# One VectorE operation for a row tile's 1448 scores instead of two in a decoder layer's cross-attention

## The reference, cut to what matters

```python
Q = (input_Q @ W_Q.T + b_Q)...            # 16 heads of 64
K = (input_K @ W_K.T + b_K)...            # 1444 keys
V = (input_V @ W_V.T + b_V)...
scores = jnp.einsum('bhqd,bhkd->bhqk', Q, K) / np.sqrt(D_K)
scores = jnp.where(attn_mask[:, None, :, :], -10000.0, scores)
attn = jax.nn.softmax(scores, axis=-1)
out = jnp.einsum('bhqk,bhkd->bhqd', attn, V)
```

## Time and profile before

| | us |
|---|---|
| median of 3 runs | 1603.62 |
| lowest, highest | 1602.78, 1609.25 |
| the profiled execution's own time | 1606.2 |
| its span, first to last instruction | 1604.5 |
| TensorE busy in the span | 1463.2 |
| VectorE busy | 1143.5 |
| ScalarE busy | 883.8 |
| GpSimd busy | 973.1 |

### The profile page before, as it was taken

One profiled execution on the slowest core, in us unless ns is written; L12 is line 12 of the kernel. 1 busy time (PEld: TensorE's weight loads), 2 busy tenths in 40 slices (PEclk: granted clock), 3 DMA queues, 4 the chain that ended last, 5 costly groups with the idle time before them and its releaser, 6 DMA issues. The chain is left out here.

```text
span 1604.5 us, 35506 instructions
## 1 busy us (share of the span) xinstructions
PE 1463.2 (91%) x10557; PEld 1408.8 (88%) x10557; DVE 1143.5 (71%) x2672; ACT 883.8 (55%) x1632; POOL 973.1 (61%) x1101
## 2 busy tenths in 40 slices
PE   4856999999999999999999999999999999956796
PEld 4736999999999999999999999999999999945585
DVE  5644878686878687868686868686868686768565
ACT  0303656565656565656565656565656565625453
POOL 2015858575857585757675767576757585414564
PEclk9956999999999999999999999999999999966898
DMA  7021111111111111111110111011101011024422
GB/s 164 1 68 62 54 34 52 35 50 35 52 35 50 35 52 35 50 36 50 35 55 31 52 34 55 31 54 32 55 31 55 30 33 35 8 65 113 113 61 88
DMA packets 98038, 80.76 MB, mean 50 GB/s; under 512 B 17577, under 2 KB 96530, under 8 KB 97714
## 3 DMA queue, kind: packets, MB, share of 16 engines
q1 hardware_dynamic: 88848, 71.83, 15.1%
q10 hardware_dynamic: 6882, 2.21, 1.0%
q0 software_dynamic: 2112, 4.29, 0.8%
HBM read 67.26 MB, written 11.04 MB: 49 GB/s over the span
## 5 line engine op out<-in xcount | busy, mean ns | idle before, releaser
L943 ACT CAST pT_hi<-banks 128x512 fp32r<-128x512 f32 (+1 forms) x672 | 360.9, 542 | 342.6 <-PE banks L1098 337.5
L1012 DVE TENSOR_TENSOR pT_lo<-banks,pT_hi 128x512 fp32r<-128x512 f32 (+1 forms) x576 | 358.2, 626 | 220.3 <-ACT pT_hi L943 212.4
L875 POOL TENSOR_SCALAR probs<-probs,row_inv 128x1408 f32<-128x1408 f32 x192 | 278.7, 1451 | 235.7 <-DVE row_inv L1004 235.4
L1098 PE MATMUL banks<-ident,probs 128*128 128x128 f32 (+1 forms) x2304 | 365.8, 274 | 5.3 <-POOL probs_half L877 3.2
L1128 PE MATMUL banks<-pT_hi,ctx_hi 128*128 128x256 f32 (+1 forms) x1056 | 329.5, 312 | 17.8 <-DVE pT_lo L1012 13.8
L863 POOL TENSOR_SCALAR bias<-mask,c_cur 128x1444 f32<-128x1444 uint8 x192 | 282.9, 1473 | 82.4 <-DVE nmax L997 64.3
L934 ACT ACTIVATE probs<-probs,nmax 128x1448 f32<-128x1448 f32 x192 | 289.8, 1509 | 39.0 <-DVE nmax L997 38.9
L1128 PE MATMUL banks<-pT_hi,ctx_lo 128*128 128x256 f32 (+1 forms) x1056 | 303.1, 287 | 0.0
L1128 PE MATMUL banks<-pT_lo,ctx_hi 128*128 128x256 f32 (+1 forms) x1056 | 302.4, 286 | 0.0
L1098 PEld LDWEIGHTS banks<-ident,probs 128*128 128x128 f32 (+1 forms) x2304 | 271.0, 140 | 17.0 <-DVE pT_lo L1012 9.0
L1082 PE MATMUL banks<-ctxT_hi,qh 128*128 128x362 f32 x832 | 241.9, 372 | 4.8 <-POOL ql L912 2.8
(11 more groups left out here) (287 smaller groups left out, 2339.9 us busy)
## 6 DMA issues: line engine op xcount, KB each, us to landing
mask<-in_mask_BxSxS_bk SPq DMA_DIRECT2D x192, 180.5 KB
nat<-in_ctx SPq DMA_DIRECT2D x16, 704.0 KB
up_raw<-in_L_ffn_W SPq DMA_DIRECT2D x32, 128.0 KB, 2.7
xs_dram<-empty SPq DMA_DIRECT2D x1, 2600.0 KB, 8.2
rows<-xs_dram SPq DMA_DIRECT2D x10, 260.0 KB, 3.0
down_raw<-in_L_ffn_W SPq DMA_DIRECT2D x16, 128.0 KB, 3.1
t_both<-yk_dram SPq DMA_DIRECT2D x3, 512.0 KB, 5.3
mask_half<-in_mask_BxSxS_bk SPq DMA_DIRECT2D x16, 90.2 KB
```

Source lines behind the costliest of these rows:

```text
L875: pool.tensor_scalar(prob(j)[0:n, 0:FIRST], prob(j)[0:n, 0:FIRST], rinv[0:n, s:s + 1], 1.0, ALU.mult, ALU.mult)
L943: act.copy(pT_hi[tslot(i, j)][:, 0:w], banks[:, T_BANK + j % 2, 0:w]).then_inc(turned_hi, 1)
L1012: dve.tensor_tensor(p_lo, turn, p_hi.bitcast(F32), ALU.subtract).then_inc(turned_lo, 1)
L1098: last = pe.transpose(banks[0:m, T_BANK + j % 2, at_col:at_col + 128], prob(t)[:, c0:c0 + m], ident[:, :])
```

## The change

`period()` puts both halves of a tile's scores next to each other, in the middle of a thirteenth of the period, instead of at even distances. `dve_order()` has one score operation per tile, at the place of the second half. It waits for the second half's scores, reads banks 0 to 3 in one instruction (four runs of 362), writes 1448 probabilities and the minimum at once, and raises `scores_taken` by 2. Nothing else is edited: ScalarE's exp waits for the same count and takes the same `nmax[:, 1]`. GpSimd's bias and normalizing keep their offsets from the halves.

```diff
@@ period()
-    for n in range(2 * NT):
-        out.append(((n + 0.5) / (2 * NT), "score", 0, n))
+    for t in range(NT):
+        for half in range(2):
+            out.append(((t + 0.5 + half / 1000) / NT, "score", 0, 2 * t + half))
@@ dve_order()
-        if kind == "score":
+        if kind == "score" and j % 2:
             out.append((n + 0.2, "score", db, j))
-            if j % 2:
-                out.append((n + 3.6, "recip", db, j // 2))
+            out.append((n + 3.6, "recip", db, j // 2))
@@ VectorE's program
                         if kind == "score":
-                            t, half = j // 2, j % 2
+                            t = j // 2
                             n, s = rows_of(t), slot(t)
-                            if half == 0:
-                                wait(dve, bias_ready, b + db, NT, t + 1)
...
+                            wait(dve, bias_ready, b + db, NT, t + 1)
...
-                            else:
-
-                                wait(dve, scores_taken, b + db, 2 * NT, j)
...
                             wait_apart(dve, scores_ready, b + db, 2 * NT, j + 1, passed_dve)
-                            cs = slice(half * 2 * CW, (half + 1) * 2 * CW)
-                            src = banks[0:n, S_BANK + 2 * half:S_BANK + 2 * half + 2, 0:CW]
-                            first = -PAD if half == 0 else nmax[0:n, 0, s:s + 1]
 
                             dve.tensor_tensor_reduce(
-                                prob(t)[0:n, cs].rearrange("p (a k) -> p a k", a=2), src,
-                                bias[(t + i) % 2][0:n, cs].rearrange("p (a k) -> p a k", a=2), -1.0, first,
-                                ALU.add, ALU.min, nmax[0:n, half, s:s + 1]).then_inc(scores_taken, 1)
+                                prob(t)[0:n, 0:SKP].rearrange("p (a k) -> p a k", a=4),
+                                banks[0:n, S_BANK:S_BANK + 4, 0:CW],
+                                bias[(t + i) % 2][0:n, :].rearrange("p (a k) -> p a k", a=4), -1.0, -PAD,
+                                ALU.add, ALU.min, nmax[0:n, 1, s:s + 1]).then_inc(scores_taken, 2)
```

More of the change, by code:

```diff
@@ L977, in emit @@
                         if kind == "score":
-                            t, half = j // 2, j % 2
+                            t = j // 2
                             n, s = rows_of(t), slot(t)
-                            if half == 0:
-                                wait(dve, bias_ready, b + db, NT, t + 1)
[L983 to L986, removed]
-                                else:
-                                    wait(dve, turned, b + db, NSTEP, steps_to(group_of(t + PSLOTS)) - NSTEP)
+                            wait(dve, bias_ready, b + db, NT, t + 1)
+                            if t >= FT:
+                                wait(dve, turned, b + db, NSTEP, 0)
+                            elif t >= PSLOTS:
+                                wait(dve, turned, b + db, NSTEP, steps_to(group_of(t - PSLOTS)))
                             else:
-                                wait(dve, scores_taken, b + db, 2 * NT, j)
+                                wait(dve, turned, b + db, NSTEP, steps_to(group_of(t + PSLOTS)) - NSTEP)
                             wait_apart(dve, scores_ready, b + db, 2 * NT, j + 1, passed_dve)
-                            cs = slice(half * 2 * CW, (half + 1) * 2 * CW)
-                            src = banks[0:n, S_BANK + 2 * half:S_BANK + 2 * half + 2, 0:CW]
-                            first = -PAD if half == 0 else nmax[0:n, 0, s:s + 1]
                             dve.tensor_tensor_reduce(
-                                prob(t)[0:n, cs].rearrange("p (a k) -> p a k", a=2), src,
-                                bias[(t + i) % 2][0:n, cs].rearrange("p (a k) -> p a k", a=2), -1.0, first,
-                                ALU.add, ALU.min, nmax[0:n, half, s:s + 1]).then_inc(scores_taken, 1)
+                                prob(t)[0:n, 0:SKP].rearrange("p (a k) -> p a k", a=4),
+                                banks[0:n, S_BANK:S_BANK + 4, 0:CW],
+                                bias[(t + i) % 2][0:n, :].rearrange("p (a k) -> p a k", a=4), -1.0, -PAD,
+                                ALU.add, ALU.min, nmax[0:n, 1, s:s + 1]).then_inc(scores_taken, 2)
                         elif kind == "recip":
```

## The result

The changed kernel takes 1827.37 us (median of 4 runs, 1825.18 to 1827.94), the kernel before 1603.6; the ratio is 1.138 [1.136, 1.141]. It was forecast slower at 1894, range 1800 to 1935: right in sign, 67 us too high.

What follows compares the result with a forecast made beforehand. TensorE's instruction stream bounds the kernel. 15 full periods at 18.5 us (277), plus 20 for the first batch, minus 7 at back edges: +290 on 1606.2 is 1896; the runs' median is 2.6 lower, 1894 us, range 1800 to 1935.

Steps and rivals of the forecast that it cites:

- The path: Attention stage: TensorE's stream sets the time; the chain score operation, exp, copy, subtraction, transpose has no slack.
- the walk: One period followed in the new order, each engine in order: TensorE waits at tiles 0 to 12 sum to 19.5 us.
- The three limits: After a tile's scores: next scores wait until 2.07 us, second-next step's transposes 2.76 (last group 2.56), one further 4.94 (4.58).
- The banks: Score banks between tiles: three steps (3.2 us) cover their 2.07 us; only tile 12 would wait, 0.15.
- The first batch: Its first four tiles have no steps beside them and wait 2.07 each: about 6, rest 14, together 20 us.
- One full period: Walk's 19.5 us less about 1 us of idle swallowed: 18.5 us per period, 15 periods, 277 us.
- the back edges: Loop's back edge: TensorE is absent 2.3 us anyway while others catch up, giving 7 x -1 us.
- About 1 us of today's idle: Each full period: idle already there that the new waits swallow, taken off the walk's 19.5 us.
- (a): Loop: granted clock falls, a tenth of TensorE's 78 us per period at 1.2 GHz; adds 60 to 120 us; chance 0.08.
- (b): Only the last group's tiles stall, preps' bank and pair waits hidden by slack: about 1700, 1650 to 1795 us; chance 0.08.
- (c): No change: three steps cover the bank wait and nothing else matters; 1595 to 1612 us, chance 0.01.
- (d): VectorE's saved 0.3 us per tile shortens what TensorE waits for: 1598 us, chance 0.01.

Runs made afterwards that it cites:

- experiment 1: Kernel before with only the new score order, both halves paired, keeping two VectorE operations per tile: 1834.94 us, 1.140.
- kernel 2: Changed kernel with the score halves back at the even distances of before, keeping the one long operation: 1759.31 us, 1.093.
- Experiment 3: Changed kernel with exp one place later in ScalarE's order: 1750.85 us, 1.085.
- experiment 5: Changed kernel with a score operation half as long, half the probabilities left out, ScalarE filled up by a copy of constants: 1701.68 us, 1.057.
- 11: Kernel before with halves paired, two operations per tile, and prep rounds 2, 5, 8 (6, 9) later: 1816.21 us, 1.129.
- 6: Changed kernel with halves 0.3 of a tile's share apart and exp one place later: 1686.59 us, 1.045.
- 10: Changed kernel with halves 0.3 of a share apart, exp one place later, and prep rounds 2, 5, 8 (6, 9) later: 1737.05 us, 1.076.
- 4: Changed kernel with the score halves 0.3 of a tile's share apart, exp as before: 1745.37 us, 1.086.
- 9: Kernel before with only exp one place later on ScalarE: 1642.46 us, 1.019.

## Why the prediction was right in direction and 67 us too high

**The path.** TensorE's stream was the bound and got longer by waits for subtractions queued on VectorE behind the operation and behind exp, as forecast. Which part of the change does it, the prediction left to its walk of the whole, and my reading of that walk, that it is the operation's length, isn't borne out: with the halves paired, two operations cost the same (experiment 1, 1.140 against 1.138).

**The operation:** 1.66 us forecast, 1661 ns measured. **VectorE's saving** was to be 60 us beside TensorE and worth nothing. It was worth nothing. The groups of the score operation and its reads add up to 423 us before (185.1 + 173.9, for the last tile 15.3 + 14.4, reads 31.9 + 2.4) and to 362 after (318.9, 26.4, reads 17), 60 less as forecast, while the busy union fell by 35 and the other groups kept their durations. So I take 25 us of the 60 to have been overlap: a read starts before its operation's end (702.37 + 0.97 = 703.34 against 703.26 in the earlier trace rows), and rows subtracted from a busy total take such overlap off twice.

**The three limits** were right where the rows show them: T + 2.07 for the release of exp and banks, T + 2.50 (2.56) for turn 39, T + 4.56 (4.58) for turn 40. **The banks** weren't the cost of the change (6.0 us), as steps in other banks stand behind the scores. The rule of the Trainium skill's Perfetto Trace Analysis (Optimizing Tensor Performance, Matmuls), that independent groups should rotate through banks, didn't decide the time here. That holds for this order alone: kernel 2 does wait for its banks, 94 us. **The first batch:** 20 forecast; the second batch's first scores start at 223.53 instead of 207.68 us, 15.8 later. (The 19.8 above is read a part of a period further on, at the projection, and is no measure of this term, close as it comes.)

**One full period: 18.5 forecast, 14.0 measured.** This is the term that was mis-sized, by 4.5 x 14 = 63 us. And there are 14 of them, not 15: the last batch has no preps for a next one beside it, and from its first scores (1534.74 instead of 1322.58 us) to the end of the span the change cost 9.1 us, where 18.5 was counted. Against these stand the 7 us that the back edges were to give back; the seven periods that hold one grew by 13.9, the seven others by 14.1, so they gave back 0.2 each. In sum 4.2 + 63 + 9.4 - 7 is 69 to 70 us, which is what the forecast of +290 had over the spans' 221.3.

Where in the period, I measured from the end of one tile's pair of scores to the start of the next, in a period away from the back edge, and set it beside the walk's (the unit times of what stands between, and the wait):

| after tile | measured | walk | | after tile | measured | walk |
|---|---|---|---|---|---|---|
| 0 | 5.60 | 5.7 | | 7 | 5.13 | 5.03 |
| 1 | 5.63 | 5.53 | | 8 | 6.14 | 6.76 |
| 2 | 4.85 | 4.83 | | 9 | 3.82 | 3.67 |
| 3 | 2.96 | 2.92 | | 10 | 5.58 | 6.08 |
| 4 | 6.56 | 6.84 | | 11 | 6.56 | 7.05 |
| 5 | 5.33 | 5.29 | | 12 | 2.11 | 2.76 |
| 6 | 4.58 | 4.57 | | | | |

Seven tiles agree within 0.1. (In the other period of a pass tile 0 has 6.1 to 8.2 and tile 12 mostly 2.9 to 3.7, since it holds the back edge.) The walk is too high at 8, 10, 11 and 12, by 2.3 in all, mostly where VectorE arrives late and the lateness is carried on. I had let each instruction start after the end of the one ahead; in the rows above two pT_hi copies of 0.43 take 0.73 together and two subtractions of 0.49 take 0.89, so queued instructions overlap by 0.1, and a chain of late ones catches up. That this is what made these four tiles shorter is argued, not shown. The other nine tiles cancel out (0.1), and a pair of halves took 2.08 instead of 2.14 (13 x 0.06 = 0.8): 3.0 found tile by tile.

The rest is in what I subtracted. "About 1 us of today's idle" was the busy share's gap in the earlier trace rows and the waits of the earlier trace rows. Unit times (an estimate) give another number: 26 halves 28.1, 30 steps of 256 columns, five of them shorter, 30.95, the last group's twelve 8.4, eleven preps 4.85, the projection 3.5; with 1.2 for the back edge 77.0. So the kernel before, at 80.0, idled about 3 us a period beside the back edge. And the walk's stalls on top of 77.0 give 96.5 where 93.0 was measured: the walk was 3.5 too high, of which the tiles above show 3.0. A busy union hides it, as the timeline of the kernel before shows at a wait for ctxT_lo:

```profile
725.79 0.49 PE L1082 MATMUL banks<-ctxT_lo,qh 128*128 128x362 f32 x2
...
726.12 0.49 PE L1082 MATMUL banks<-ctxT_hi,ql 128*128 128x362 f32 x2
...
726.86 0.39 PE L1128 MATMUL banks<-pT_hi,ctx_hi 128*128 128x256 f32 x1 [0.25 <-DVE ctxT_lo L1038]
```

The last pair of score matmuls starts at 726.12 and is followed 0.74 us later, where 0.33 would do: 0.41 lost, and the row shows 0.25, since the pair's modelled tail of 0.49 covers the rest. The change's longer stalls swallow about 2 us more of such idle than I took off. 3.5 + 2 = 5.5, which is the forecast 18.5 less the 13.0 of these two periods (over all fourteen, 4.5). This sum closes whatever the unit times are; how it splits rests on the 77.0, and only the 3.0 of the tiles was found apart from it.

**Which waits:** pT_lo first, then oT_lo and qf at the preps, banks small, as forecast. Experiment 3 shows that exp's place ahead of the copy is a third of the loss, experiment 5 that an operation of half the length takes away over half of it; as the table shows, such shares overlap and aren't to be added.

**Signs that missed.** A period of 96 to 98 us was to show, and it is 93.6. TensorE was to be busy near 80% of the stage, and the window has 87%: I had counted its work as a stream, and a busy total counts a matmul's tail before each wait too.

**Rivals.** (a) A falling clock: not as a cost of the change. The loop's mean is 0.99 before and after, with 5 and 6 short falls. What I had overlooked is that it fell in the kernel before, behind the 2.3 us gap at the back edge. The mean was lower in kernels 11, 6, 1 and 10 (0.96, 0.97, 0.98, 0.98), though by less than the tenth of the work at 1.2 GHz that the rival took. (b) Only the last group's tiles stall: fell, tiles 5 to 8 and 10 stall as the walk has them. (c) and (d), no change or faster, fell: TensorE's stream is the bound and got longer.

**The step I would have got wrong** is not in the prediction but in the expectations behind it: I took the causes as additive. Five of those expectations (1, 2, 4, 9, 10) were too low, and in 1, 4 and 10 the lists show other waits in the place of those taken away.

**Open.** Why the clock falls behind some waits and not behind others of the same length: of the changed kernel's twelve waits of 1.85 us from 240 to 1400 us three were followed by a fall, of kernel 1's twelve of 2.2 us ten. Why the operation alone costs more than a walk gives. Why later preps cost 50 us in kernel 10: that VectorE's pair and so ql come late is argued from the waits list, not shown by a run. How much of 5's gain is the earlier result, how much VectorE's shorter work, how much ScalarE's. Why GpSimd holds TensorE in kernel 1.

## What to carry to other kernels

Merging two operations saves time on the engine that runs them, but whoever waits for either one now waits for the whole; where that engine isn't the bound, the saving may be worth nothing, so list for each in-order queue what stands behind the merged operation and who on the bound engine needs it. A merge often needs its inputs moved together, and that move is to be priced by itself: here it cost 14% with the operation merged or not. Such stalls sit in shared queues and move: a remedy for one wait is to be tried whole, not added up from parts. And a list of waits and a busy share leave out idle time: add up unit times over a period and compare with the period. A mean over periods hides that the first and the last are of another kind, and a mean clock hides short falls.

## What the runs showed of the hardware that was not expected

A wait of 2.22 us, in a loop in which TensorE was 86% busy (kernel 1), was followed by three windows of 2 us at a lowered granted clock, 0.50 at its lowest, and one of 1.85 us in the changed kernel, at 87%, by 0.89, 0.50 and 0.75, while most of that kernel's waits of the same length were followed by no fall. The means over the loop, 0.98 and 0.99, hardly show it. The operation over four banks in one instruction costs per element what one over two does: 907 ns for 724 elements, 1661 for 1448, or 1.04 ns an element and 0.15 us fixed by these two; taken from four banks with 181 columns each, 724 elements took 911. Instructions that are queued on ScalarE or VectorE run into each other by about 0.1 us.
